# Windowed attention and top-1 experts on one core: the rows' transfers spread out, the experts' preparation and first group moved, the values' product changed from split to plain fp32

## What is computed

```python
scores = zeros; scores[window blocks] = (q k^T) * scale; scores[global rows, global rows] += (gq gk^T) * scale
attn   = softmax(scores, axis=-1);  x = layernorm(x + (attn @ v) @ wo.T + bo)
h      = gelu((xhat * s_e + b_e) @ W1_e + b1_e);  y = sum_e (top1 == e) * (h @ W2_e + b2_e);  x = layernorm(x + y)
```

## Time and profile before

| | |
|---|---|
| time, median of 3 runs (range) | 478.96 us (476.92 to 480.76) |
| the profiled execution: time, span | 478.51 us, 477.0 us |
| PE busy | 431.9 us, 91% |
| PEld, DVE, ACT, POOL busy | 368.7, 325.4, 242.1, 236.0 us |
| chain that ended last | PE 78%, DVE 12%, issue 4%, ACTq 2%, ACT 2% |
| mean granted clock | 0.972 |

### The profile page before, as it was taken

How to read it: one execution, slowest core, us unless ns; L and a number is a source line. 1 busy time by engine, 2 the same in 40 slices (tenths; PEclk the granted TensorE clock), 3 DMA queues, 4 the chain that set the end, 5 groups by cost and what they waited for, 6 DMA issues and landing times.

```text
span 477.0 us, 15500 instructions
## 1 busy us (share of the span) xinstructions
PE 431.9 (91%) x6027; PEld 368.7 (77%) x6039; DVE 325.4 (68%) x824; ACT 242.1 (51%) x533; POOL 236.0 (49%) x327
## 2 busy tenths in 40 slices
PE   2779899999999999999999999887979998998981
PEld 1766788888888888888888888765757887877871
DVE  5494966576576576576666775746574888899776
ACT  0533356656556556556556556457544564544320
POOL 3043153654654645645645546535523575477441
PEclk9989899999999999999999999989789999999997
DMA  8702345000000000000000000100000011011112
GB/s 244 254 14 58 124 156 172 26 15 13 22 12 11 22 11 11 22 11 11 22 11 12 25 14 1 47 1 3 1 0 1 2 46 44 0 44 44 45 45 89
DMA packets 21962, 20.37 MB, mean 43 GB/s; under 512 B 3373, under 2 KB 21922, under 8 KB 21922
## 3 DMA queue, kind: packets, MB, share of 16 engines
q1 hardware_dynamic: 17684, 15.60, 10.3%
q10 hardware_dynamic: 4238, 4.22, 2.7%
HBM read 15.41 MB, written 4.41 MB: 42 GB/s over the span
## 4 chain that ended last, share of the span: by engine, by line
PE 78%; DVE 12%; issue 4%; ACTq 2%; ACT 2%; DVEq 0%; POOL 0%; POOLq 0%
PE ps L1287 20%; PE ps L1318 10%; PE ps L1598 8%; PE ps L1327 7%; PE ps L1575 7%; PE ps L1341 6%; PE ps L1309 4%; PE ps L1347 4%; PE ps L1508 3%; PE ps L1332 2%; ACTq L675 2%; DVE row_max_t L1093 1%; PE ps L1354 1%; PE ps L1385 1%; DVE hm_part L1238 1%
## 5 line engine op out<-in xcount | busy, mean ns | idle before, releaser
L1093 DVE TENSOR_REDUCE row_max_t<-ps 128x16 f32<-128x2048 f32 x32 | 73.3, 2292 | 64.6 <-PE ps L1318 64.6
L809 ACT ACTIVATE probs<-ps 128x1024 f32<-128x1024 f32 x64 | 62.1, 1022 | 28.2 <-PE ps L1332 28.2
L1287 PE MATMUL ps<-xT,wT 128*128 128x128 f32 x512 | 67.1, 285 | 1.1 <-ACT x_part L681 1.1
L1287 PEld LDWEIGHTS ps<-xT,wT 128*128 128x128 f32 x512 | 61.3, 196 | 7.9 <-issue 6.6
L1598 PE MATMUL ps<-w_part,hm_part 128*128 128x256 f32 x384 | 54.9, 292 | 3.8 <-DVE hm_part L1238 3.3
L593 POOL TENSOR_TENSOR attn_t<-num_t,rden_t 128x256 f32<-128x256 f32 x32 | 19.9, 622 | 77.8 <-DVE rden_t L1120 77.8
L1575 PE MATMUL ps<-xh_part,w_part 128*128 128x512 f32 x192 | 55.1, 424 | 0.0
L1598 PEld LDWEIGHTS ps<-w_part,hm_part 128*128 128x128 f32 x384 | 48.6, 192 | 6.6 <-DVE hm_part L1238 3.9
L1318 PEld LDWEIGHTS ps<-k_part,q_part 32*128 32x128 f32 x1584 | 47.0, 186 | 7.2 <-issue 6.9
L1318 PE MATMUL ps<-k_part,q_part 32*128 32x128 f32 x1584 | 51.5, 274 | 1.1 <-issue 1.0
L556 POOL TENSOR_TENSOR q_part<-qf,q_part 128x512 fp32r<-128x512 f32 x32 | 41.3, 1290 | 18.3 <-ACT q_part L681 18.3
(11 more groups left out here) (214 smaller groups left out, 895.1 us busy)
## 6 DMA issues: line engine op xcount, KB each, us to landing
table<-rest_sums SPq DMA_DIRECT2D x4, 1088.0 KB, 6.0
xs<-in_L_attn_x_dram SPq DMA_DIRECT2D x32, 128.0 KB, 2.0
rows<-in_L_attn_x_dram ACTq DMA_DIRECT2D x4, 1024.0 KB, 11.8
out_dram<-yout SPq DMA_DIRECT2D x7, 512.0 KB, 2.8
w<-in_L_ffn_W_dram SPq DMA_DIRECT2D x2, 256.0 KB, 4.1
w<-in_L_ffn_W_dram SPq DMA_DIRECT2D x1, 512.0 KB, 3.8
out_dram<-yout SPq DMA_DIRECT2D x2, 256.0 KB, 2.1
w_raw<-in_L_attn_wq_dram SPq DMA_DIRECT2D x1, 256.0 KB, 2.8
```

Of the source, the lines that this page charges most:

```text
L809: act.activation(probs[:, 2 * h:2 * h + 2, :], ps[:, 2 * h:2 * h + 2, :], ACT.Exp).then_inc(probs_ready, 1)
L1093: dve.tensor_reduce(row_max[:], ps_all, op=ALU.max, axis=AX.X).then_inc(max_ready, 1)
L1287: last = mm(out, lhsT(c), rhs(c), start=(c == 0), stop=(c == KC - 1))
```

## The change

It has four parts.

1. **Rows' transfers.** The first activation and `xgT` come ahead of the four 1 MB transfers, and each of these is issued at a place of its own in ACT's start-up (`load_rows(0)` to `(3)`). W1's two transfers move on SP's queue ahead of the output bias and of x(2).
2. **Values.** One plain fp32 product from `xT` and `wT` (2 matmuls, which the profile counts as 4) in place of 6 fp32r ones; `x_part`, `wv_part` and what ACT and POOL did for them are gone.
3. **Experts' preparation.** The bias product goes into TensorE's start-up and `b1s` with it; `gate` and `rank` to step 24; `split_first_layer` in three pieces to steps 25, 26 and 27; `stack_second_bias` to step 31; `factors` of the last 12 windows takes four instructions per quarter over two expert steps.
4. **First group.** Everything of group 0 one step earlier (scaled in 29, turned in 30, logits, `route` and low parts in 31, one-hot in 32), and the first two quarters of its first layer in step 33, on ACT with gelu and high part. The second layer's weights are copied in step 34.

```diff
@@ ACT, start-up
-            for i in range(ROUNDS):
-                act.dma_start(rows_v[...i...], x_w[...i...]).then_inc(ld_x[i], 16)
             act.wait_ge(pool_const, 1)
             act.activation(e_val[:, 0, :], zeros16[:], ACT.Exp)
+            def load_rows(i): ...
             copy(xgT[:]..., ps[:, 5, 0:HID]).then_inc(xgT_ready, 1)
+            load_rows(0)
...
             turned_x(0, 0)
+            load_rows(1)
...
-            weight_high(0, wv_part)
             queries_of(0, 0)
+            load_rows(2)
...
             values_of(0, 0)
+            load_rows(3)
@@ POOL
-                if ahead:
-                    x_low(t + AHEAD, p)
@@ PE, values and start-up
-            def values_of(w):
-                pe.wait_ge(x_low_ready, w + 1)
-                split_product(ps_kv[:, HID:2 * HID], x_part, wv_part).then_inc(v_in_psum, 1)
+            def values_of(w, p):
+                product(ps_kv[:, HID:2 * HID], lambda c: xT[:, p, c, :], lambda c: wT[:, WV, c, :]).then_inc(v_in_psum, 1)
...
             product(ps_pv[:, 0:HID], ...).then_inc(bias_in_psum, 1)
-            values_of(1)
+            pe.wait_ge(ld_w1, 16 * KC)
+            for f in range(FC):
+                last = product(ps_pv[:, HID + f * EPC:HID + (f + 1) * EPC], ...w1..., ...vecT...)
+            last.then_inc(b1_in_psum, 1)
+            values_of(1, 1)
@@ PE, step
+                if not steady and t == NW + 1:
+                    pe.wait_ge(probs_ready, 2 * NW)
+                    first_layer(0, 0, 0)
...
                 if not steady and t == NW + 1:
-                    turn_onehot(0)
-                    ...the bias product...
+                    first_layer(0, 0, 1)
@@ ACT, step
+                if not steady and t == NW + 1:
+                    for c in range(2):
+                        hidden(0, 0, c)
+                        hidden_high(0, 0, c)
@@ DVE, step
-                if not steady and t == 0:
-                    split_first_layer()
-                if not steady and t == 1:
+                if not steady and t == FACTORS_AT:
+                    gate_columns()
+                if not steady and FACTORS_AT < t < FACTORS_AT + 4:
+                    split_first_layer(t - FACTORS_AT - 1)
+                if not steady and t == NW - 1:
                     stack_second_bias()
-                if not steady and t == NW - 1:
+                if not steady and t == NW - 2:
                     ...take_high(0, 0, pair)
-                if not steady and t == NW:
+                if not steady and t == NW - 1:
                     ...route(k, 0), then the low parts
@@ DVE, expert step
-                    if not steady and n == 0:
-                        factors(EARLY, NW, c * 7, min(c * 7 + 7, FACTOR_STEPS))
+                    if not steady and n < 2:
+                        k = FC * n + c
+                        factors(EARLY, NW, min(4 * k, FACTOR_STEPS), min(4 * k + 4, FACTOR_STEPS))
```

More of the change, by code:

```diff
@@ L296, in windowed_attention_then_top1_experts @@
         b1_in_psum = sem("b1_in_psum")
+        w1_ready = sem("w1_ready")
         gs_in_psum = sem("gs_in_psum")
@@ L764, in evacuate, with hidden, hidden_high @@
                     scale_rows(n + 1, pair)
+            def hidden(n, p, c):
+                need(act, hm_low_ready[c // 2], 2 * (n - 1) + c % 2 + 1)
+                if isinstance(n, int) and n == 0 and c == 0:
+                    act.wait_ge(ffn_w_ready, 1)
+                act.wait_ge(h_in_psum, 4 * n + c + 1)
+                act.activation(hT[:, c, :], ps[:, c, :], ACT.Gelu, bias=b1s[:, c:c + 1]).then_inc(h_ready, 1)
+            def hidden_high(n, p, c):
+                need(act, y_in_psum, 4 * (n - 1))
+                act.wait_ge(h_ready, 4 * n + c + 1)
+                copy(hm_part[0][:, p, c, :], hT[:, c, :]).then_inc(hm_high_ready, 1)
             def keep_logits(n):
@@ L822, in step @@
                     queries_of(t + AHEAD, (s + AHEAD) % SLOTS)
-                if not steady and t == NW - 2:
+                if not steady and t == NW - 3:
                     act.wait_ge(centred, EARLY)
@@ L1000, in _ @@
             dve.wait_ge(ld_bo, 16)
+            dve.wait_ge(b1_in_psum, 1)
+            for k in range(EPC):
+                part = slice(k * EH, (k + 1) * EH)
+                last = dve.tensor_tensor(b1s[part, :], ps[part, 7, HID + k:HID + EPC * FC:EPC], b1[part, :], ALU.add)
+            last.then_inc(ffn_w_ready, 1)
             dve.tensor_tensor(out_bias[:], ps_pv[:, 0:HID], out_bias[:], ALU.add).then_inc(out_bias_ready, 1)
@@ L1304, in _ @@
             SPLIT = ((0, 0), (1, 0), (0, 1))
-            def split_product(out, rows_part, w_part):
-                terms = [(a, b, c) for a, b in SPLIT for c in range(KC)]
-                for i, (a, b, c) in enumerate(terms):
-                    last = mm(out, rows_part[a][:, c, :], w_part[b][:, c, :], start=(i == 0), stop=(i == len(terms) - 1))
-                return last
             def scores(s):
@@ L1434, in values_of_rest, with first_layer @@
                 last.then_inc(v_rest_in_psum, 1)
+            def first_layer(n, p, c):
+                if c == 0:
+                    if isinstance(n, int) and n == 0:
+                        pe.wait_ge(w1_ready, 1)
+                    pe.wait_ge(high_ready, 2 * n + 2)
+                    pe.wait_ge(low_ready, 2 * n + 2)
+                need(pe, h_ready, 4 * n + c - 3)
+                terms = [(k, a, b) for k in range(KC) for a, b in SPLIT]
+                for i, (k, a, b) in enumerate(terms):
+                    mm(ps[:, c, :], w1_part[a][:, k, c * P:(c + 1) * P],
+                       xh_part[b][:, p, k, :], start=(i == 0), stop=False)
+                if c == 0:
+                    pe.wait_ge(ohT_ready, n + 1)
+                mm(ps[:, c, :], others_off[:, c, :], ohT[:, p, :], start=False, stop=True).then_inc(h_in_psum, 1)
             def step(t, s, steady=False):
```

124 lines of the change are left out of this document (40 added, 84 removed).

## The result

The changed kernel takes 477.88 us (median of 20 runs, 475.53 to 479.27), the kernel before beside it 480.15 (476.92 to 484.04): ratio 0.995, interval 0.993 to 0.997. The forecast was 472.0 with a range of 466.5 to 477.5. The change gains 2.3 us where 6.6 to 7 were forecast. The profiled execution of the changed kernel took 478.04, its span is 476.3.

What follows compares the result with a forecast made beforehand. TensorE was taken to bound the kernel, busy nine tenths of the span, with DVE and POOL nearly as long in steady steps. Terms -6.1 + 0.4 - 1.5 + 0.3 + 0.5 - 0.2 = -6.6 gave 472.0 us, range 466.5 to 477.5.

Steps and rivals of the forecast that it cites:

- The transfers, -6.1: Start: without ACT's four issues in the way, TensorE's first products start at 8.45 in place of 14.52, gaining 6.1 us.
- it shifts as a whole: Start: the path from first products to the values of window 1 is unchanged work and moves earlier with them, by 6.1.
- The bias product, +0.4: Start: it takes 2.36 us where TensorE waited 1.80 before the values of window 1; cost 0.4, bounds 0 and 0.6.
- W1's split out of step 0, -1.5: Step 1: without it the row maxima end before TensorE asks; gain 1.5, bounds -1.2 and -2.5.
- The split in steps 25 to 27, +0.3: Three pieces of at most 1.3 us go into DVE's 2.01 us hole; cost 0.3, bounds 0 and 2.
- The values, +0.5: fp32 values cost 0.15 more per window, wholly covered in steady steps, uncovered in the first three; bounds 0 and 4.8.
- Rival B: Attention steps: the fp32 values are not covered, 0.07 to 0.15 per window, up to 476.3 (478 by the skill); chance 0.12.
- The end of attention, -0.2: Handover to experts: first layer 2.7 earlier, mostly given back, plus a longer stretch at 1.2 GHz; bounds -4 and +5.
- route of group 1 ... returns about 2.2: Handover: eight factors in place of 14 stand ahead of the one-hot TensorE waited 2.41 for; about 2.2 comes back.
- One first-layer product costs 1.5 more: Handover: TensorE idles about 3 us in step 32, lengthening the 1.2 GHz stretch, where one such product costs 1.5 more.
- C: Handover: DVE's queue in step 31, ACT's in step 33 and the slow clock cost 5, giving 477; chance 0.11.
- D: Step 31: DVE is locked out beside POOL, 16 small instructions putting 17 us ahead of num_t, giving 489; chance 0.06.

Runs made afterwards that it cites:

- x5: x4 with five extra unused matmuls in TensorE's idle time at the start, ahead of the values of window 1; 467.23 us, ratio 0.971 to the kernel before.
- x4: The changed kernel with the second bias's DVE instructions back in step 1 from step 31; 469.26 us, ratio 0.9774 to the kernel before.
- x2: The kernel before with the values change alone (one fp32 product, no split); 479.66 us, ratio 0.9972 to the kernel before.
- x8: x4 with the first layer of group 0 left wholly to the expert steps again; 468.13 us, ratio 0.9725 to the kernel before.
- x9: x4 with DVE's factor instructions of the last windows moved behind the one-hot of group 1; 467.82 us, ratio 0.9716 to the kernel before.
- x10: The "best version": x4 with x5's and x9's edits, last aT_t ahead of ACT's second gelu, W2's split in step 33; 459.84 us, ratio 0.957.
- x15: x10 with the second bias back in step 31, where the change has it; 466.08 us, ratio 0.970 to the kernel before.
- x17: x10 with sum_windows() in place of the unused matmuls ahead of the values of window 1; 458.14 us, ratio 0.9538 to the kernel before.
- x14: x10 with W2's high and low parts (its split) back behind attention; 462.83 us, ratio 0.962 to the kernel before.
- x16: x15 with five extra unused matmuls in step 32, ahead of the wait for residual_t; 463.21 us, ratio 0.964 to the kernel before.
- x13: The changed kernel with five extra unused matmuls in step 32, behind the wait for residual_t; 477.46 us, ratio 0.992 to the kernel before.

## Why the prediction was wrong

**The transfers, -6.1: right.** First products at 8.51, issues of 0.37 to 0.48; alone it is worth 6.3 us (interval 4.0 to 8.8). What failed is a sentence behind it, "it shifts as a whole". TensorE's own work did, but the slow stretch took a new place and length. Against the profiled execution of before the maxima of step 3 moved by 4.2 where -6.1 + 0.4 - 1.5 = -7.2 were forecast; against its second profile, with the slow stretch in the like place, by 9.5. I took one execution for the kernel. How much of the 6.1 reaches the end therefore differs between executions; the table's rows and the interval above are all that is shown of it.

**The bias product, +0.4: too small to tell.** It took 1.84, all ahead of DVE's `k_part`, with 2.33 of idle time left, so no cost of its own shows.

**W1's split out of step 0, -1.5: right in kind, its size not shown.** The turned scores of window 0 at 51.28 have no wait. From maxima 0 to maxima 3 it takes 32.3 before and 30.1 in x5, but before the granted clock was 0.71 from 53 to 57 and 0.86 to 61, behind the wait of 1.25, so the 2.2 is not the split's alone; no run takes out this part by itself.

**The split in steps 25 to 27, +0.3: right.** Maxima 24 to 31 take 60.46 in the second profile of before and 60.55 in x4, all at full clock. (The first profile has 61.49 with its slow stretch at 310; the changed kernel 60.95.)

**The values, +0.5: right**, with the cover whole: x2 and every steady step. Rival B is out.

**The end of attention, -0.2: this step failed.** From the maxima of window 31 to the end it is 164.9 against 161.2 and 159.7 in the two profiles of before: +3.7 to +5.2, at the upper bound. Up to the third quarter my count was nearly right. `num_t` of window 30 comes at 324.26, on the old times 328.7: 2.5 later, as forecast. The third quarter was put at 344.5 on the old times, or 340.0 with the 4.5 gained by then, and it stands at 341.06. What failed is the last line, "route of group 1 ... returns about 2.2": from the third quarter to the one-hot it takes 9.28 in place of 7.57, so 1.7 more where 2.2 less was forecast. That misses by 3.9, as much as the whole term does against the first profile.

I counted the factors ahead of the one-hot (eight for fourteen) and not what POOL does beside them. Measured from the maxima of window 31, the one-hot is 4.0 later than before, and DVE's rows give the parts: the high part of group 1 starts 3.1 later, it lasts 2.1 longer (2.57 for 0.43), and the factors return 1.2, not 2.2. The six that are gone took about 0.2 each; the four long ones, 1.2 each beside POOL's instructions, are there in both kernels.

Why DVE's high part meets POOL's instruction: that instruction comes 1.75 behind the residual of window 31 in both kernels. The high part came 4.5 behind the residual before, since TensorE had a first-layer quarter ahead of turning group 1, and comes 1.9 behind it now, since that quarter stands earlier. The second bias has no part in this: x4, without its delay, has the same overlap (2.43 us). The first layer does: with it late again (x8) the high part comes 2.9 behind the residual and lasts 1.53.

The one-hot is waited for 4.66, forecast below 0.5. TensorE's next quarter is slow behind it (2.86), but so it was before (2.52): from the one-hot to the end both take about 126. Where the wait was 0.6 or less (x4, x9, x10, x15, x17) it is 124.4. x14 prices POOL's instruction at 3.0, x9 the factors at 1.4.

I also priced the second bias by its length, and the clock behind it too low. The bias costs 7.5 from the maxima of window 31 to the end (x4), of which 6.0 stand at the one-hot already and 1.6 are the slow stretch that in x4 fell ahead of the one-hot. In the best version it costs 6.2, of which 2.9 is the clock behind TensorE's idle time (x16). The idle time itself I forecast at about 3, and it was 2.66. "One first-layer product costs 1.5 more" was a single instruction group of a stretch that covers three of them.

**Rivals.** C (handover worse by 5, 477) came closest in place and size, at a chance of 0.11. D had the right mechanism at the wrong place: the lock-out is small in step 31, where POOL works only from 317.93 to 319.39 of that time (the eleven instructions take 4.3 in place of 3.4), and large in expert step 0, yet far below the 17 us of its sum. The Trainium skill (SBUF — State Buffer, SBUF: two separate sides) calls this an exclusive lock for whole instructions: by it DVE's high part, issued second and in a fast mode, would end right behind POOL's instruction. The trace agrees, 343.27 against 342.98, though no run shows the mode.

## What to carry to other kernels

A wait of TensorE can cost, beside its length, a slow stretch behind it, unless something else covers that stretch: mark the longer idle times and ask what runs behind them. Fill them with work that the kernel has to do anyway (x17), and see that it stands ahead of the wait, not behind it (x13). Before counting instructions in front of a due one on DVE, read what POOL does in the same microseconds. And profile the kernel before twice when its times spread by more than the gain that is looked for.

## What the runs showed of the hardware

- One program has its slow stretch at different places in different executions: queries and keys of window 1 took 3.46 us in one profile of before and 2.02 in the other, `sum_windows` 3.64 and 6.06. The Trainium skill (TensorE: Matmul & The Clock Gate, What's actually happening) says that the number of slow matmuls varies between runs of one kernel, and the traces agree. The slow stretch at the end of attention costs 2.9 us of 466 (x15 against x16). At the start, filling the idle time moves the maxima of step 3 by 4.5 us and the median time by 2.0 (x5 against x4).
- The clock fell behind an idle time of 2.33 us at the start of the changed kernel (0.50 from 27.5), and did not in x17, where that time was filled. Not every such wait has a slow stretch behind it: behind the 1.71 at 337.60 in the changed kernel the granted clock stays 1.00.
- A DVE instruction on 128x12 values takes 0.17 us alone and 1.19 to 1.25 beside POOL's; a cast of 128x512 takes 0.43 alone and 2.57 beside POOL's 2.40 (2.43 beside 2.37 in x4).
